# Linear attention's second product with swapped operands in four column tiles

## What is computed

```python
q, k, v = heads(x, Wq, bq), heads(x, Wk, bk), heads(x, Wv, bv)      # 16 heads of 16
qp = relu(q @ rw) + 1e-6                                            # 64 features per head
kp = relu(k @ rw) + 1e-6
kv   = einsum('bhsf,bhsd->bhfd', kp, v)
qkv  = einsum('bhsf,bhfd->bhsd', qp, kv)
norm = einsum('bhsf,bhf->bhs', qp, kp.sum(axis=2))
attn = (qkv / (norm[..., None] + 1e-6)) @ Wo + bo
x1 = layernorm(x + attn)
y  = silu(x1 @ Wg + bg) * (x1 @ Wu + bu) @ Wd + bd                  # 1024 hidden
y += product-key experts: route x1, keep the 8 best of 1024 per head (4 heads),
     weights softmax(scores) * silu(x1 . down), summed over up
out = layernorm(x1 + y)
```

## Time and profile before

| | |
|---|---|
| median of 3 runs | 3632.07 us (3629.95 to 3634.01) |
| profiled execution | 3635.19 us |
| its span, first to last instruction | 3633.4 us |
| mean granted TensorE clock | 0.991 of full |
| busy: PE, PEld, DVE, ACT, POOL | 98%, 81%, 71%, 55%, 42% of the span |
| matrix product records | 19420 |

### The profile page before, as it was taken

One profiled execution on the slowest core, in us unless ns is written; L12 is line 12 of the kernel. 1 busy time (PEld: TensorE's weight loads), 2 busy tenths in 40 slices (PEclk: granted clock), 3 DMA queues, 4 the chain that ended last, 5 costly groups with the idle time before them and its releaser, 6 DMA issues.

```text
span 3633.4 us, 52250 instructions
## 1 busy us (share of the span) xinstructions
PE 3549.2 (98%) x19420; PEld 2929.1 (81%) x19420; DVE 2585.7 (71%) x5554; ACT 1981.3 (55%) x2886; POOL 1514.3 (42%) x1012
## 2 busy tenths in 40 slices
PE   8789999999999999999999999999999999999988
PEld 6668888888888888888888888888888888888877
DVE  4577777777777777777777777777677777777773
ACT  4455465555555555556555555555655554555551
POOL 0354344443344434444433444443444434555440
PEclk9899999999999999999999999999999999999999
DMA  3000000000000000000000000000000000000000
GB/s 118 18 12 18 13 13 12 18 18 12 12 18 12 18 18 13 12 18 13 18 18 13 13 13 18 18 14 17 13 12 18 18 7 12 13 13 12 7 6 12
DMA packets 23339, 61.17 MB, mean 17 GB/s; under 512 B 5552, under 2 KB 10032, under 8 KB 23088
## 3 DMA queue, kind: packets, MB, share of 16 engines
q1 hardware_dynamic: 18480, 41.04, 3.6%
q0 software_dynamic: 4608, 16.78, 1.1%
HBM read 41.04 MB, written 16.78 MB: 16 GB/s over the span
## 4 chain that ended last, share of the span: by engine, by line
PE 90%; DVE 3%; ACT 3%; POOL 1%; issue 1%; SPq 0%; DMA 0%; DVEq 0%; ACTq 0%; POOLq 0%
PE ring L639 28%; PE y_bank L732 12%; PE y_bank L734 11%; PE step_bank L554 6%; PE step_bank L562 6%; PE step_bank L666 6%; PE step_bank L639 5%; PE step_bank L598 3%; PE step_bank L656 3%; PE step_bank L548 3%; PE step_bank L590 3%; PE step_bank L712 3%; PE y_bank L728 1%; POOL grid L461 1%; DVE prob L1120 1%
## 5 line engine op out<-in xcount | busy, mean ns | idle before, releaser
L461 POOL TENSOR_TENSOR grid<-ex 128x1024 f32<-128x1024 f32 x512 | 1066.3, 2090 | 999.2 <-DVE prob L1117 364.3
L732 PE MATMUL y_bank<-wd_sb,gate 128*128 128x256 f32 x2048 | 621.6, 385 | 0.0
L734 PE MATMUL y_bank<-up_sb,wexp 128*128 128x256 f32 x2048 | 609.1, 379 | 0.0
L1107 DVE SCALAR_TENSOR_TENSOR grid<-grid,best 128x1024 f32<-128x1024 f32 x256 | 329.0, 1285 | 328.2 <-POOL grid L461 327.3
L1120 DVE SCALAR_TENSOR_TENSOR prob<-grid,narrow,prob 128x1024 f32<-128x1024 f32 x256 | 450.7, 1760 | 7.9
L639 PE MATMUL ring<-x1T_hl,downT_hl 128*128 128x512 f32 x1536 | 421.3, 409 | 17.2 <-ACT gate L883 17.2
L639 PE MATMUL ring<-x1T_hl,wg_hl 128*128 128x512 f32 x1536 | 428.8, 414 | 3.1 <-DVE gate L1136 3.1
L734 PEld LDWEIGHTS y_bank<-up_sb,wexp 128*128 128x128 f32 x2048 | 389.1, 190 | 52.8
L639 PE MATMUL ring<-x1T_hl,wu_hl 128*128 128x512 f32 x1536 | 422.2, 410 | 0.0
L732 PEld LDWEIGHTS y_bank<-wd_sb,gate 128*128 128x128 f32 x2048 | 354.0, 190 | 50.8 <-issue 22.7
L883 ACT ACTIVATE gate<-ring,bg_sb 128x512 f32<-128x512 f32 x256 | 176.3, 689 | 396.7 <-PE ring L639 395.0
(11 more groups left out here) (159 smaller groups left out, 5920.9 us busy)
## 6 DMA issues: line engine op xcount, KB each, us to landing
xb<-in_L_attn_x SPq DMA_DIRECT2D x34, 512.0 KB, 3.7
out_y<-x POOLq DMA_DIRECT2D x32, 512.0 KB, 3.0
xa<-in_L_attn_x SPq DMA_DIRECT2D x30, 512.0 KB, 3.7
prob<-in_L_ffn_down_embed SPq DMA_DIRECT2D x1, 1024.0 KB, 5.8
prob<-in_L_ffn_Wg SPq DMA_DIRECT2D x1, 1024.0 KB, 8.6
prob<-in_L_ffn_Wu SPq DMA_DIRECT2D x1, 1024.0 KB, 10.5
wd_sb<-in_L_ffn_Wd SPq DMA_DIRECT2D x1, 1024.0 KB, 11.4
up_sb<-in_L_ffn_up_embed SPq DMA_DIRECT2D x1, 1024.0 KB, 12.1
```

The source lines that it names most:

```text
L461: pool.tensor_tensor(grid[:, h % 2], bcast(ex[:, h, 0:NX].unsqueeze(2), [P, NX, NK]), bcast(ex[:, RH + h, 0:NK].unsqueeze(1), [P, NX, NK]) ...
L732: pe.matmul(rows, gate[:, c % 2, t * P:(t + 1) * P], wd_sb[:, c, :], start=(c == 0 and t % 2 == 0), stop=False, skip_group_check=True)
L734: mm = pe.matmul(rows, wexp[:, c % 2, t * P:(t + 1) * P], up_sb[:, c, :], start=False, stop=(c == C - 1), skip_group_check=True)
L1107: marks["keep", h] = rt_steps.mark(dve.scalar_tensor_tensor(out=g, in0=g, scalar=best[:, h, TOP - 1:TOP], in1=g, op0=ALU.is_ge, op1=ALU.mult))
```

## The change

The second product swaps its operands: kv_blocks becomes the stationary one, 32 columns (two heads of 16) for each head pair, and qp the moving one, 512 tokens. Four head pairs write to partitions 0, 32, 64 and 96 of one bank. Numerators (`num`) and denominators (`den`) are separate products with separate matrices; the denominators' matrix repeats each head's sum 16 times, so that both results have the same shape: 128 features of attention by 512 tokens, already transposed. `back` is gone. ACT evacuates den with the constant added, DVE inverts the whole 128 x 512 tile in place and multiplies with the numerators.

The epsilon that POOL added to qp becomes a constant per output row (epsilon times the column sum of the matrices), computed once per batch by 16 products with a column of -0.5 (`consts_use`, at step 1) and two DVE operations. v is stored without its bias; bv goes through Wo into bo once at the start, and enters the constants as -epsilon times bv. attnT moves from qp's memory to x1's, wo's sum goes to xb, norm1 writes x1. SP's load of xb now waits for norm1 (`x1_ready`), and SP issues the store in place of POOL. The order of the uses and the planner's entries change with it.

```diff
-    AT_SEQ = ([("turn", 0), ("turn", 1), ("q", 0), ("q", 1)] + [("qp", j) for j in range(4)] + [("qkv", 0)]
-              + [("qp", 4), ("qp", 5), ("qkv", 1), ("qp", 6), ("qp", 7), ("qkv", 2), ("qkv", 3)]
-              + [("back", 0), ("back", 1), ("wo", 0), ("wo", 1), ("next", 0), ("next", 1)])
+    AT_SEQ = ([[("turn", 0)], [("turn", 1)], [("q", 0)], [("q", 1)]] + [[("qp", j)] for j in range(4)] + [[]]
+              + [[("den", 0), ("num", 0)], [("divide", 0), ("qp", 4)]] + [[("qp", j)] for j in range(5, 8)] + [[]]
+              + [[("den", 1), ("num", 1)], [("divide", 1)], [], [("wo", 0)], [("wo", 1)], []])
...
+        AT_EARLY, AT_MID, AT_LATE = ([AT_SEQ[3 * c + k] for c in range(C - 1)] for k in range(3))
+        AT_EARLY.append([]), AT_MID.append([]), AT_LATE.append([("next", 0), ("next", 1)])
...
-        WORK = {"turn": 0.44, "k": 1.73, "q": 1.73, "v": 1.73, "kp": 0.47, "qp": 0.46, "qkv": 1.73, "sum": 1.73,
-                "back": 0.44, "wo": 1.73, "next": 0.44, "rt": 1.39, "pt": 0.44, "fold": 2.6, "ff": 1.39, "out": 1.73}
-        HOLD = {"turn": 2.0, "k": 6.0, "q": 6.0, "v": 4.0, "kp": 2.0, "qp": 2.0, "qkv": 3.5, "sum": 3.0,
-                "back": 2.0, "wo": 3.0, "next": 5.0, "rt": 8.0, "pt": 5.0, "fold": 9.0}
+        WORK = {"turn": 0.44, "k": 1.73, "q": 1.73, "v": 1.73, "kp": 0.47, "qp": 0.46, "den": 0.95, "num": 0.95, "consts": 0.6, "sum": 1.73,
+                "wo": 1.73, "next": 0.44, "rt": 1.39, "pt": 0.44, "fold": 2.6, "ff": 1.39, "out": 1.73}
+        HOLD = {"turn": 2.0, "k": 6.0, "q": 6.0, "v": 4.0, "kp": 2.0, "qp": 2.0, "den": 2.0, "num": 8.0, "consts": 2.0, "sum": 3.0,
+                "wo": 3.0, "next": 5.0, "rt": 8.0, "pt": 5.0, "fold": 9.0}
...
-                        sp.wait_ge(*drained("at", m - 1, "wo", 1))
+                        sp.wait_ge(x1_ready, m * T)
                     sp.dma_start(xb[:], x_groups[m]).then_inc(xb_loaded, 16)
+                if last:
+                    sp.wait_ge(y_ready, (f + 1) * T)
+                    sp.dma_start(out_groups[f], y_sb[:]).then_inc(y_stored, 16)
...
-                def qp_add(j):
-                    wait_apart(pool, drained("at", m, "qp", j))
-                    pool.tensor_scalar(qp[:, j % 4], qp[:, j % 4], ATTN_EPS, 1.0, ALU.add,
-                                       ALU.mult).then_inc(qp_eps, 1)
...
-                    if last and c == 1:
-                        pool.wait_ge(y_ready, (f + 1) * T)
-                        pool.dma_start(out_groups[f], y_sb[:]).then_inc(y_stored, 16)
...
+            for k in range(KD):
+                mm = pe.matmul(ring[0][:, 0:D], bv_sb[:, k:k + 1].broadcast_to([P, P]), wo_sb[:, k, :],
+                               start=(k == 0), stop=(k == KD - 1))
+            mm.then_inc(bo_full, 1)
...
+            def weights(kind, c):
+                return (num_w if kind == "num" else den_w)[:, c].rearrange("p g d -> p (g d)")
+            def consts_use(a):
...
+                for col, kind in enumerate(("num", "den")):
+                    for c in range(FC):
+                        row, at = 2 * DK * (c % 4), 2 * col + c // 4
+                        mm = pe.matmul(bank[row:row + 2 * DK, at:at + 1], weights(kind, c), neg_half[:, 0:1],
+                                       start=True, stop=True)
...
-                    elif kind == "qkv":
-                        pe.wait_ge(qp_eps, m * FC + 2 * j + 2)
...
-                        for t in range(T):
-                            for c in range(2):
-                                mm = pe.matmul(at_bank[:, (2 * t + c) * W:(2 * t + c + 1) * W],
-                                               qp[:, (2 * j + c) % 4, t * P:(t + 1) * P],
-                                               kv_blocks[:, 2 * j + c].rearrange("p a b -> p (a b)"),
-                                               start=True, stop=True)
-                    elif kind == "back":
-                        pe.wait_ge(*drained("at", m, "qkv", 2 * j + 1))
-                        mm = turn(at_bank, x1, j)
+                    elif kind in ("den", "num"):
+                        if kind == "den":
+                            for k in range(4):
+                                pe.wait_ge(*drained("at", m, "qp", 4 * j + k))
...
+                        for k in range(4):
+                            mm = pe.matmul(at_bank[2 * DK * k:2 * DK * (k + 1), :], weights(kind, 4 * j + k),
+                                           qp[:, k, :], start=True, stop=True)
                     elif kind == "wo":
-                        pe.wait_ge(*drained("at", m, "back", 1))
+                        pe.wait_ge(*drained("at", m, "num", 0))
+                        pe.wait_ge(*drained("at", m, "num", 1))
...
-                    elif kind == "back":
-                        read_by(act.copy(attnT[:, j, :], at_bank[:]), "at", m, kind, j)
+                    elif kind == "den":
+                        if last and j == 0:
+                            act.wait_ge(y_stored, (it - LAST_LAG + 1) * 16)
+                        act.wait_ge(*drained("kv", batch * BG - 1, "consts", 0))
+                        read_by(act.activation(attnT[:, j, :], at_bank[:], ACT.Identity,
+                                               bias=consts[:, 2 + j:3 + j]), "at", m, kind, j)
...
-                        at_steps.mark(dve.tensor_scalar(den[:], heads[:, :, :, DK], ATTN_EPS, None, ALU.add))
...
-                        at_steps.mark(dve.reciprocal(den[:], den[:]))
...
-                        read_by(dve.tensor_tensor(rows, heads[:, :, :, 0:DK],
-                                                  bcast(den[:].unsqueeze(3), [P, T, 4, DK]),
-                                                  ALU.mult), "at", m, kind, j)
+                    elif kind == "divide":
+                        rows = attnT[:, j, :]
+                        dve.wait_ge(*drained("at", m, "den", j))
+                        at_steps.mark(dve.reciprocal(rows, rows))
+                        at_steps.wait()
+                        dve.wait_ge(*full("at", m, "num", j))
+                        dve.wait_ge(consts_ready, batch)
+                        read_by(dve.scalar_tensor_tensor(out=rows, in0=bank_of("at", m, "num", j)[:],
+                                                         scalar=consts[:, j:j + 1], in1=rows, op0=ALU.add,
+                                                         op1=ALU.mult), "at", m, "num", j)
```

## The result

The changed kernel takes 3732.94 us (median of 4 runs, 3725.51 to 3734.92) where the kernel before takes 3632.39 beside it (3629.95 to 3634.01). The ratio is 1.0274 [1.0256, 1.0291]: slower, where 3532 was forecast. The profiled run took 3725.51 us.

What follows compares the result with a forecast made beforehand. TensorE was taken to bound the kernel: 256 us removed, 132 and 13 added, 11 of waits, so 3635 - 111 + 11 = 3535, 3532 as a median of runs. The range was 3505 to 3612, chance 0.82.

Steps and rivals of the forecast that it cites:

- What bounds the kernel: Whole run: TensorE, busy 3549.2 of 3633.4 us, so work leaving it shortens the run nearly one for one.
- den and num at 2.06 us a pair: TensorE's den and num products: four column tiles stream at once, 1.72 + 0.34 us a pair, 132 us in all.
- Rivals 3 to 5: TensorE's den/num pair: strict order, 3669 us, chance 0.09; two tiles at a time, 3641, 0.06; no overlap, 3862, 0.03.
- The rule of program order: TensorE: products start and end in strict program order, so a den/num pair takes nine rounds of 0.43 us, 4.2 with 0.34.
- The constants on TensorE: TensorE, once per batch: 16 one-column products at 1.5 us, eight times 12 us; 13 us with the one-off bv product.
- First failed step: TensorE's constants, once per batch: placed one step after VectorE makes the blocks, they should find them ready; no wait booked.
- Second failed step: First divide on VectorE: pushes the next tile's choice and exponential back; 3 us booked for the 28 full groups.
- The list of what would show the forecast wrong: Signs: pairs of 3.4 us or more, L562 waiting for each divide, a wait for xb, or for a bank behind num.
- The second divide: VectorE, behind keep(2,2), with TensorE's wo(0) waiting: the tight place, 2.2 us short in the last four groups, 9 us.
- The reciprocal: VectorE's divide: 6.25 ns per element, so 3.35 us for 512 elements per partition; bounds 0.74 and 4.5 us.
- Rival 2: VectorE's divides become the wait, reciprocal a third longer: 32 to 80 us more, 3565 to 3610 us, chance 0.12.
- xb's load and store: SyncE: xb's load waits for norm1 with 5 us or more of cover, the store follows it; no cost booked.

Runs made afterwards that it cites:

- e5: Changed kernel with the constants' reader in step 1 and both divides moved ahead of the gate product ff_h on VectorE: 3511.48 us, ratio 0.966.
- e11: e5 with each den use issuing its four products twice: 3558.74 us.
- e1: Changed kernel with the two VectorE operations that read the constants' bank in step 1 instead of step 2: 3663.75 us.
- e7: e5 without e1's edit, so both divides moved and the constants' reader left late: 3583.69 us.
- e9: e1 with only the first divide (step 3) moved ahead of ff_h on VectorE: 3536.39 us.
- e10: e1 with only the second divide (step 5) moved ahead of ff_h on VectorE: 3643.73 us.

## Why the prediction was wrong, and where it was right

- **What bounds the kernel:** right for before. After, it no longer was TensorE alone, and e5, where it is again, shows that the step was not one of balance.
- **den and num at 2.06 us a pair: right.** The pair takes 1.85 us and the product behind it 1.58 against 1.40: 2.03. The records start in fours: in the changed kernel's pair four between 1644.49 and 1644.52, none until 1644.94, then the next four. Rivals 3 to 5 wanted 3.6 us and more and are excluded, by e11 too. The rule of program order, from the Trainium skill ("TensorE: Matmul & The Clock Gate", "The mechanism"), isn't seen here: under it a pair would take nine rounds of 0.43 us where it takes 1.85 us, and a doubled den four rounds more where e11 shows two.
- **The constants on TensorE: too dear.** 32 records took 0.43 us; I had booked 1.5, at eight times 12 us. By price that is 9 us and the pair's 0.03 us makes 2, about the 10 us by which e5 (3511) lies under the forecast without its waits, 3532 - 11 = 3521. That it comes out so well is partly luck. By the sum's prices a steady iteration should lose 3.9 us and it lost 4.4 (108.93 to 104.53), and a late one lost only 2.5 (95.35 to 92.82). The cause of these differences wasn't traced.
- **First failed step: "Its wait for the blocks stands one step after VectorE makes them, so it should find them ready."** That is true and beside the point. I costed TensorE's side of the constants alone, and never asked who empties their bank, behind what that reader stands, and who gets the bank next. The term was put at nothing and measures 69 (e1) or 72 us (e7).
- **Second failed step: "The first divide, one step pair earlier, pushes the next tile's choice and exponential back by up to that much, so I book 3 us".** The first divide measures 127 us (e9), against 3 booked. I followed what hangs on its result, and of the bank behind it I wrote that the plan gives num back "later than that by 1 to 2 us". But the 9 us for which I took num to be held counted no wait of VectorE for keep: it is 12. And the next reader in the queue, kv_sum's addition, I didn't name at all; it gives the larger of the two waits. The list of what would show the forecast wrong did name a wait of TensorE for a free bank behind num, but no term of the sum and no rival priced it. What the waits bring with them, 44 us more busy time in products that didn't change, has no term either.
- **The second divide: the right place, twice too small.** It was called the tight place, with 9 us; e10 gives 20, in the 6 groups that the waits show. It was tight, but it was not the place that mattered. (The two bookings, 3 and 9 us, add up to 12 and not 11.)
- **The reciprocal: right.** 6.25 ns an element, taken from 4 and 16 elements, gave 3.35 us; the rows show 3.35. A divide is 4.1 us.
- **Rival 2** came nearest: the divides did become the wait. Its place (wo in each group), its cause (a steeper slope) and its price (32 to 80 us) were off; it is 147 to 152, and the constants' wait, which no rival had, takes it over the line to slower. Together e5 + 152 + 69 = 3733, which closes by construction, as each step is the difference of two runs; e7 (72 for the constants, against 69) shows that the two losses are nearly independent.
- **At no cost, right:** xb's load and store. TensorE waits 5.6 us for xb in all of e5 and 6.0 in e9, against 4.0 in the kernel before.

The gain that was forecast is there and the change gives it back and as much again nearly: 121 us in e5 against 221 us lost to two places in VectorE's queue.

## What to carry to other kernels

Price an added operation by its place in its engine's in-order queue as well as by its length: the same 4.1 us, twice a group, cost some 150 us a run behind a wait of VectorE and next to nothing inside it. Where banks are handed out by a plan, follow each bank to its reader, to what that reader stands behind, and to the next user of the bank, even for work done eight times in a run. If TensorE's waits name a reader instead of a producer, move the reader before touching the plan of banks.

## What the runs showed of the hardware

- Four column tiles stream float32 products side by side; a pair of 16 records takes 1.85 us, and 8 records more 0.86. Coming in and going out costs 0.3 us a pair (1.85 against 1.72, and 1.58 against 1.40 behind it), as with the two tiles of the earlier trace rows.
- Products of one column are nearly free in the four column tiles: 32 records in 0.43 us, 13 ns each.
- When VectorE and GpSimd start on 128x1024 within 0.05 us of each other, one of the two takes 3.0 us and the other its usual 1.28 or 1.90. In the changed kernel L1144 (the steady timeline above) starts at 1632.55 and takes 3.03 us, GpSimd's L464 at 1632.59 takes 1.90. In the kernel before, at the same place, it was GpSimd that took 3.00 and VectorE 1.28:

```profile
1590.26 1.28 DVE L1120 SCALAR_TENSOR_TENSOR prob<-grid,narrow,prob 128x1024 f32<-128x1024 f32 x1
```

```profile
1590.31 3.00 POOL L461 TENSOR_TENSOR grid<-ex 128x1024 f32<-128x1024 f32 x1 [1.34 <-DVE prob L1117]
```

In the kernel before there are 128 such meetings: 66 times VectorE is the slow one, 62 times GpSimd. In the changed kernel and in e5 it is VectorE all 128 times, and away from a meeting its operation takes 1.3 us. Over the run the mean of this operation of VectorE rose with the change (changed kernel, groups by line and shape; 1760 ns before), though nothing in it was touched:

```profile
L1144 DVE SCALAR_TENSOR_TENSOR prob<-grid,narrow,prob 128x1024 f32<-128x1024 f32 x256 | 552.0, 2156 | 9.0
```

It stays at 2156 in e5, so it costs little where VectorE has room. In the changed kernel it stands between the divide and kv_sum's addition and so makes that reader later; no run took it out. Why the slower one changed sides (GpSimd has fewer additions to do now, and comes on time) was only argued, not tried.
